# Attention of an adaLN block: slots of four heads at a time, with the probabilities turned by VectorE blocks and DRAM transfers instead of TensorE transposes

## The reference, cut to what matters

```python
mod = (silu(c) @ wmod).reshape(B, 6, 1, -1)          # sa, ca, ga, sb, cb, gb
h = layernorm(x) * (1 + ca) + sa
# attention: q, k with rotary embedding, causal softmax
scores = jnp.einsum('bhtd,bhsd->bhts', q, k) * (1.0 / np.sqrt(HD))
scores = jnp.where(tril, scores, -jnp.inf)
att = jax.nn.softmax(scores, axis=-1)
out = jnp.einsum('bhts,bhsd->bhtd', att, v)
x = x + ga * (out.transpose(0, 2, 1, 3).reshape(B, T, H * HD) @ wo)
h = layernorm(x) * (1 + cb) + sb
x = x + gb * (silu(h @ w1.T + b1) * (h @ w2.T + b2) @ w3.T + b3)
```

## Time and profile before

| | |
|---|---|
| median of 3 runs | 897.12 us (895.2 to 897.33) |
| the profiled execution, span from first to last instruction | 892.2 us |
| difference of the two (what lies around the span) | 4.9 us |
| TensorE (PE) busy | 870.8 us, 98% of the span |
| VectorE (DVE) busy | 590.9 us, 66% |
| ScalarE (ACT) busy | 509.9 us, 57% |
| GpSimd (POOL) busy | 465.4 us, 52% |
| moved by DMA | 38.22 MB, 43 GB/s on average |

### The profile page before, as it was taken

How to read it: one execution, slowest core, us unless ns; L and a number is a source line. 1 busy time by engine, 2 the same in 40 slices (tenths; PEclk the granted TensorE clock), 3 DMA queues, 4 the chain that set the end, 5 groups by cost and what they waited for, 6 DMA issues and landing times.

```text
span 892.2 us, 14536 instructions
## 1 busy us (share of the span) xinstructions
PE 870.8 (98%) x4716; PEld 744.8 (83%) x4716; DVE 590.9 (66%) x1693; ACT 509.9 (57%) x1194; POOL 465.4 (52%) x362
## 2 busy tenths in 40 slices
PE   8899999999999999999999999999999999998897
PEld 2798888888888888888888888888888887876786
DVE  4957756576656565666666565766565656788886
ACT  3657656575647475656656565756474656544410
POOL 1755745284537554563557462845475544525542
PEclk9999999999999999999999999999999999999999
DMA  9710101010101010101001010101010100111011
GB/s 330 229 46 1 60 1 60 1 61 1 59 0 59 0 59 0 35 24 51 8 0 59 0 59 0 59 0 59 0 47 0 71 1 26 58 72 24 1 48 47
DMA packets 27663, 38.22 MB, mean 43 GB/s; under 512 B 2416, under 2 KB 11760, under 8 KB 27632
## 3 DMA queue, kind: packets, MB, share of 16 engines
q1 hardware_dynamic: 27216, 37.76, 12.6%
q10 hardware_dynamic: 416, 0.07, 0.0%
HBM read 35.73 MB, written 2.10 MB: 42 GB/s over the span
## 4 chain that ended last, share of the span: by engine, by line
PE 90%; DVE 6%; ACT 2%; issue 1%; DMA 1%; SPq 0%; ACTq 0%; DVEq 0%
PE x_bank L311 27%; PE q_bank L311 19%; PE s_row L311 14%; PE o_bank L387 13%; PE t_col L373 6%; PE s_row L373 1%; PE s_row L611 1%; PE t_col L622 1%; PE q_bank L611 1%; PE x_bank L611 1%; DVE wo_raw L916 1%; DVE attn_lo L850 1%; PE x_bank L321 1%; PE x_bank L339 1%; DMA wmod_sb<-in_L_wmod_dram 1%
## 5 line engine op out<-in xcount | busy, mean ns | idle before, releaser
L1225 POOL TENSOR_TENSOR q_tmp<-q_tmp,sin_sb 128x512 f32<-128x512 f32 x64 | 87.6, 1369 | 274.4 <-ACT q_tmp L996 274.4
L987 ACT ACTIVATE probs<-probs,neg_max 128x128 f32<-128x128 f32 (+3 forms) x256 | 140.9, 561 | 4.0 <-DVE neg_max L673 2.1
L951 ACT ACTIVATE pT_hi<-t_col 128x512 fp32r<-128x512 f32 x128 | 69.6, 596 | 128.1 <-PE t_col L373 128.1
L668 DVE CUSTOM_DVE_ANT_0 probs<-s_row,mask_sb 128x256 f32<-128x256 f32 (+3 forms) x256 | 115.0, 486 | 4.1 <-issue 0.5
L694 DVE TENSOR_TENSOR attn_lo<-o_bank,attn_hi 128x512 fp32r<-128x512 f32 x64 | 44.2, 691 | 108.4 <-ACT attn_hi L951 108.3
L1203 POOL TENSOR_TENSOR qT_lo<-q_tmp,qT_hi 128x512 fp32r<-128x512 f32 x63 | 82.0, 1301 | 55.7 <-ACT qT_hi L951 55.7
L311 PE MATMUL q_bank<-hT_hi,wq_hi 128*128 128x512 f32 x256 | 105.3, 411 | 1.5 <-DVE q_tmp L658 1.5
L951 ACT ACTIVATE attn_hi<-o_bank 128x512 fp32r<-128x512 f32 x64 | 38.4, 599 | 119.6 <-PE o_bank L387 119.6
L311 PE MATMUL q_bank<-hT_hi,wq_lo 128*128 128x512 f32 x256 | 100.2, 392 | 0.0
L311 PE MATMUL q_bank<-hT_lo,wq_hi 128*128 128x512 f32 x256 | 100.2, 391 | 0.0
L311 PE MATMUL x_bank<-wo_hi,attn_hi 128*128 128x512 f32 x240 | 93.7, 390 | 0.1
(11 more groups left out here) (295 smaller groups left out, 2124.2 us busy)
## 6 DMA issues: line engine op xcount, KB each, us to landing
wo_raw<-in_L_attn_wo_dram SPq DMA_DIRECT2D x8, 1024.0 KB, 5.3
wq_raw<-in_L_attn_wq_dram SPq DMA_DIRECT2D x7, 1024.0 KB, 5.8
wmod_sb<-in_L_wmod_dram SPq DMA_DIRECT2D x6, 512.0 KB, 8.1
wmod_sb<-in_L_wmod_dram SPq DMA_DIRECT2D x3, 1024.0 KB, 13.5
wk_raw<-in_L_attn_wk_dram SPq DMA_DIRECT2D x8, 256.0 KB, 5.2
wv_raw<-in_L_attn_wv_dram SPq DMA_DIRECT2D x8, 256.0 KB, 6.0
wq_raw<-in_L_ffn_w_dram SPq DMA_DIRECT2D x2, 1024.0 KB, 5.3
out_dram<-acc SPq DMA_DIRECT2D x8, 256.0 KB, 2.1
```

What stands on the lines that cost most here:

```text
L668: last = nc.vector.tensor_tensor_reduce(probs[:, s, ROW_AT[i]:ROW_AT[i] + ROW_W[i]], s_out[i], mask_sb[:, T - ROW_W[i]:T], 1.0, LOWEST, AL ...
L951: nc.scalar.activation(dst, src, ACT.Copy).then_inc(done, 1)
L987: last = nc.scalar.activation(span, span, ACT.Exp, bias=neg_max[:, s, i:i + 1], scale=SCALE, accum_out=row_sum[:, s, i:i + 1])
L1225: nc.gpsimd.tensor_tensor(b, b, sin_sb[:, :], ALU.mult).then_inc(q_sin, 1)
```

## The change

A **slot** takes the place of the step: one tile of 128 queries, for all four heads of a group, of one batch entry. There are still 8 slots in a group and 64 in all; the query tiles come in the order 0, 3, 1, 2.

- **Scores.** q is stored as [dimension, block of 32 tokens, head, 32], so that the 128 stationary columns of a score matmul are 32 queries of each of the four heads. A slot has four such matmul triples, for the four blocks of 32 queries, against 32(4i+t+1) keys: the causal edge is cut at 32 columns instead of 128. The maxima write `probs` as [key block of 128, key chunk of 32, query block t, 32].
- **Turning.** One VectorE transpose per slot turns every 32x32 block of the slot's probabilities (`turn_blocks`). SP then writes the blocks to a DRAM buffer with four transfers (one per head, 32 partitions each), waits for them, and reads them back with one transfer in which the keys stand on 128 partitions. The read of slot s waits until `attend` of slot s-2 has let the buffer go.
- **Attend** of slot s-3 stands in slot s: three matmuls of 512 columns (four heads by 128 queries) for each key block. The output product of slot s-4 follows it.
- **Moved between engines.** The row normalisation goes from VectorE to ScalarE. The low part of the turned probabilities goes from VectorE to GpSimd. The rotary embedding loses ScalarE's two swapping copies and GpSimd's sine product; VectorE does three products (one of 128 partitions, two of 64 that read the other half). The negated maximum comes out of the maxima instruction itself, and the small memsets go.
- **Schedule.** The loop over groups is written out. Four q projections of the first group and one of batch entry 1, all turns of x and the six modulation pieces now stand before group 0. Raw weights share their place with the low parts, the weights come in more and smaller transfers.

The core of the diff:

```diff
-            def turn_probs(g, j, final=False):
-                need(pe, probs_normed, STEPS, g, j + 1)
-                ...
-                        for i in range(jj, TT):
-                            at = ROW_AT[i] + jj * P
-                            last = pe.transpose(t_out[jj][:, (i - jj) * P:(i - jj + 1) * P],
-                                                probs[:, j % 2, at:at + P], ident[:, :])
+            def scores(g, s):
+                b, i = s // TT, tile_of(s)
+                ...
+                for t in range(QT):
+                    need(pe, rows_maxed, QT * SLOTS, g, QT * (s - 1) + t + 1)
+                    n = width(s, t)
+                    product(s_banks[t][:, 0:n], lambda a, _: qT[a][b][:, QT * i + t, :, :],
+                            lambda a, _: kT[a][b][:, 0:n], [0]).then_inc(scores_ready, 1)
+            def attend(g, s):
+                b, i, par = s % SLOTS // TT, tile_of(s), s % 2
+                need(pe, attn_lo, SLOTS, g, s)
+                ...
+                    last = pe.matmul(o_bank[:, :], v_s[a][:, b, st_, :], pT[bb][par][:, :, PLACES[par] - 1 - i + st_, :],
+                                     start=(k == 0), stop=(k == len(steps) - 1))
+            def rotate(src, ring):
+                a, b = rope_tmp[:, ring, 0, :], rope_tmp[:, ring, 1, :]
+                nc.vector.tensor_tensor(a, src[:, :], cos_sb[:, :], ALU.mult)
+                nc.vector.tensor_tensor(b[0:HALF, :], src[HALF:HD, :], sin_sb[HALF:HD, :], ALU.mult)
+                nc.vector.tensor_tensor(b[HALF:HD, :], src[0:HALF, :], sin_sb[0:HALF, :], ALU.mult).then_inc(roped, 1)
+            def turn_blocks(g, s):
+                par, i = s % 2, tile_of(s)
+                need(dve, probs_normed, SLOTS, g, s + 1)
+                need(dve, blocks_out, MOVES * SLOTS, g, MOVES * s)
+                ...
+                nc.vector.transpose(dst, src).then_inc(blocks_turned, 1)
+            def blocks_to_dram(g, s):
+                par, i = s % 2, tile_of(s)
+                need(sp, blocks_turned, SLOTS, g, s + 1)
+                need(sp, pT_in[par], 16 * TT, g, 16 * (s // 2))
+                for h in range(REP):
+                    sp.dma_start(spread[par, :, :, h, 0:(i + 1) * P].rearrange("c s n -> s c n"),
+                                 turned[W32 * h:W32 * (h + 1), :, TT - 1 - i:, :].rearrange("p c a t -> p c (a t)")
+                                 ).then_inc(blocks_out, 16)
+            def blocks_to_keys(g, s):
+                par, i = s % 2, tile_of(s)
+                need(sp, blocks_out, MOVES * SLOTS, g, MOVES * (s + 1))
+                need(sp, attn_done, SLOTS, g, s - 1)
+                sp.dma_start(pT_raw[par][:, :, PLACES[par] - 1 - i:, :].rearrange("p h a t -> p h (a t)"),
+                             spread[par, :, :, :, 0:(i + 1) * P].rearrange("c s h n -> (c s) h n")).then_inc(pT_in[par], 16)
+            def normalise(g, s):                      # ScalarE
+                par = s % 2
+                need(act, inv_ready, SLOTS, g, s + 1)
+                for t in range(QT):
+                    rows = prob_rows(s, t)
+                    last = nc.scalar.activation(rows, rows, ACT.Copy, scale=row_inv[:, par, t:t + 1])
+                last.then_inc(probs_normed, 1)
+            def probs_low(g, s):                      # GpSimd
+                ...
+                    split_lo(pT[1][par][:, :, at, :], pT_raw[par][:, :, at, :], pT[0][par][:, :, at, :], pT_lo)
-            with pe.Fori(1, KV - 1) as g:
+            for g in range(1, KV - 1):
                 group(g)
```

More of the change, by code:

```diff
@@ new lines, in project_out @@
+            def project_out(g, s, x_free=None):
+                need(pe, attn_lo, SLOTS, g, s + 1)
+                need(pe, wo_added, SLOTS, g, s - 1)
+                dst = x_bank if s % 2 else out_bank
+                for h in range(REP):
+                    if s % SLOTS == 0:
+                        need(pe, wo_lo, REP, g, h + 1)
+                    for a, bb in PARTS:
+                        last = pe.matmul(dst[:, :], attn[a][:, s % 2, h * P:(h + 1) * P], wo_s[bb][:, h, :],
+                                         start=(h == 0 and (a, bb) == PARTS[0]), stop=(h == REP - 1 and (a, bb) == PARTS[-1]))
+                last.then_inc(wo_made, 1)
@@ L874, in _ @@
             group(0, first=True)
-            with dve.Fori(1, KV - 1) as g:
+            gates()
+            group(1)
+            for g in range(2, KV - 1):
                 group(g)
             group(KV - 1, last=True)
-            probs_low(KV - 1, STEPS - 1)
-            f_low(3)
+            end = KV - 1
+            add_out(end, SLOTS - 5)
+            attn_low(end, SLOTS - 3)
             f_low(4)
-            attn_low(KV - 1, STEPS - 1)
+            x1_stats(0)
+            x1_stats(1)
@@ L903, in _ @@
             for k in range(KC):
                 h2_low(k)
-            for u in range(9, 3 * KC):
-                f_low(u)
+            add_out(end, SLOTS - 1)
+            x1_stats(TT)
+            x1_stats(TT + 1)
             x1_stats(TT + 2)
```

1192 lines of the change are left out of this document (585 added, 607 removed).

## The result

The changed kernel takes 899.4 us, the kernel before 895.0 (medians of 20 runs each); the ratio is 1.0044, 95% interval 1.0032 to 1.0057. It is slower by about 4 us, where 825 us was forecast. One of the 20 runs of the changed kernel took 1326.6 us at a mean granted clock of 0.555 and has no part in the ratio. The profiled execution has a span of 896.0 us and a run time of 897.8.

What follows compares the result with a forecast made beforehand. The prediction took PE's issue time to bound attention: 892.2 us span less 93.4 of PE work gives 798.8, plus 21 for edges gives 819.8, with 4.9 around it 825 us; own range 804 to 850, 802 to 870 with rival 1.

Steps and rivals of the forecast that it cites:

- The work on TensorE: Per slot: transposes 1.09 us, attend 0.20 and scores 0.17 come off, 11.86 to 10.40; 93.4 us over 64 slots.
- The costs of the other engines: Work per slot: VectorE 6.8 us including 1.4 for the block transpose, ScalarE 6.5, GpSimd 7.8.
- Rival 3: Block transpose at the reciprocal's price: VectorE needs 13.8 us a slot, run about 1020 us; chance 4%.
- All fit below 10.40: Loop: VectorE, ScalarE and GpSimd each have less work per slot than TensorE's 10.40 us.
- edge (c): Loop: small stalls where GpSimd or ScalarE is behind (slot 3), 1 us a group, +7 us.
- rival 1: Loop: VectorE and ScalarE hand-overs become the bound, 11.0 to 11.3 us a slot, about 865 us; chance 25%.
- Edge (a): Start: work moved ahead of the first scores costs nothing in sum, but PE waits longer for VectorE's chain, +2 us.
- Edge (b): Group 0, slots 1 to 3: no attend or output product, PE has less work than the others, +5 us.
- Edges (d) and (e): Last group's slots 3 to 6 limited by the buffer's loop, +4 us; last attend waits for a full DRAM trip, +3.
- The trip through DRAM: Probabilities stored and reloaded: 10 to 12 us from transpose to landing, hidden in the loop, nearly bare in the last group.
- rival 2: The DRAM buffer's loop from attend to attend sets the pace: slot 12.8 us, about 965 us; chance 7%.
- What was said would show it wrong: PE's middle windows well below 97% busy; GpSimd's low part fed by late DMA as releaser would name rival 2.

Runs made afterwards that it cites:

- e6: The kernel before with only 3 of the 10 transposes of the probabilities per step in groups 1 to 7: 860.9 us, ratio 0.9620.
- e11: e1 with VectorE's block transpose of each slot done twice: 935.2 us, ratio 1.0477 to the kernel before.
- e1: The changed kernel with the high and low parts of wv's second half made in slot 4 instead of slot 5: 877.1 us.
- e2: The changed kernel with 8 unread 512-column matmuls added in slot 6 while TensorE waits for wv's low part: 885.9 us.
- e4: The changed kernel with 7 unread 512-column matmuls in the wait ahead of the transposes of x at 49 us: 893.0 us.
- e14: The changed kernel with the six modulation pieces ahead of the wait for x, two unread 512-column matmuls behind each: 893.1 us.
- e3: The changed kernel with the six modulation pieces spread between the prologue's projections instead of in one row: 885.9 us.
- e7: The changed kernel with e1's and e3's edits and, in the last group, the first gate's copy ahead of wo's high parts: 865.9 us.
- e8: e7 with gate operations split over two slots, last-group gate and weight turns behind attend, and low parts ahead of the second norm's small operations: 862.8 us.
- e5: The changed kernel with a DRAM-to-DRAM copy added between store and load of the probabilities: 940.3 us, ratio 1.0517 to the kernel before.
- e10: e1 with e5's added DRAM-to-DRAM copy: 936.3 us, ratio 1.0482 to the kernel before.
- e9: e8 with VectorE's output-product sum ahead of the maxima in alternate slots, gate operations one per slot, 8 unread matmuls in the tail's wait: 860.3 us.

## Why the prediction was wrong

- **The work on TensorE: right.** 1.46 us a slot was forecast, 93.4 in all; 88.5 came off, and the steady group has 84.0 us of work where 83.2 was said. Read by starts, a group has 14.1 us of scores (14.0 forecast) and 13.6 of attend (13.6). Of the transposes 8.07 us are gone, 1.01 a step and not 1.09: the slower start behind them, 0.08 a step, was counted as gone too, but the projections and the output product take 55.6 us a group, not less than the 55.4 before. In e6 a turn is worth the 0.109 us that the forecast had.
- **The costs of the other engines: right.** The block transpose takes 1.04 ns a column (2313 ns for 2048, 1.51 us a slot against 1.4); GpSimd's 7.8 us a slot is its 70% of 11.1; VectorE and ScalarE have 7.1 and 7.2 us against 6.8 and 6.5. Rival 3 falls. The Trainium skill's 311 ns ("VectorE: DVE Perf Modes", section "The three transpose paths") is for one 128x128 turn in bf16, a point that the prediction left out; ten times that, an estimate from the page's figure, is 3.1 us a slot, and the trace has 1.51 in float32. The four widths here (712, 1246, 1778 and 2313 ns for 512 to 2048 columns) lie on 0.18 us for each instruction plus 1.04 ns a column, which would give a lone turn of 128 columns 0.31 us, an estimate from these four: the page's figure itself is not contradicted, only multiplying it by the ten blocks of a long instruction.
- **"All fit below 10.40" was the failed step**, and with it edge (c): 1 us of stalls a group, where 4.7 us were lost in a steady one (3.0 of waits and 1.7 at half clock). I compared sums of busy time with the slot, and not where each result stands in its queue. wv's low part was in my sum (part of GpSimd's 1.55 us for weights) but I never asked which slot it is made in, what stands ahead of it, and who waits: project_v in slot 6. "Each semaphore has a slot or more of slack" was said of rival 1 without a row; e11 refutes it: adding 1.5 us a slot to VectorE, busy for 66% of the time, cost 6.3 us a group. How much of the loss this step explains: the steady groups, 23.6 us of the 92 in the table above, and a part of groups 0 and 1, where the same wait for wv stands (3.35 and 2.08 us). The rest are the steps below.
- **Rival 1 hit the loop's number by luck.** It gave 11.0 to 11.3 us a slot; measured is 88.67 / 8 = 11.08. But its cause was VectorE and ScalarE waiting for each other, and what e1 and e2 show is GpSimd's low part of wv (2.07 us a group) and the clock behind it (1.7); VectorE's sum is 0.7. Its 865 has neither the clock nor the ends.
- **The clock was in no term.** The earlier trace rows showed 1.00 before, because TensorE never rested, and I carried that over to a kernel in which I forecast rests. 38 of the 76 us missed are this. In the loop the wait of slot 6 is paid almost twice (2.07 + 1.7, e1 and e2); other waits of 2.0 and 2.8 us were paid once.
- **Edge (a), the start: 2 us forecast, 17 measured** (6.4 of waits and 10.5 at half clock; the moved work itself, 19.7 us at full clock, is as forecast). "Moved work ... costs nothing in sum" is the failed sentence. The pieces cost 1.70 us each when they stood alone between wide matmuls; in one row of six they take 2.9 (17.2 / 6), whether TensorE was idle before them or not (e4, e14). Spread, 10 to 13 us come back (e3). The wait for x's norm was 6.3 us, three times what I allowed.
- **Edge (b), groups 0 and 1.** 5 us were forecast for group 0, and it has 9.7 of waits and 6.8 at half clock: rotations (0.90 and 3.12 us), q's low part (1.26) and wv (3.35). Group 1 was in no edge but (c): the gates' row of small operations on VectorE was not in the sums by slot.
- **Edges (d) and (e), the end: 7 us forecast.** The last group and tail have 26.5 us of waits, all from 740 us on (5.70, 2.00, 2.36, 1.95, 2.83, 0.67, 6.70, 1.09, 3.17), and lose 9.2 at half clock; before it was 10.2 and 1.6, so 24 us came on top. The waits are not at attend for the trip as forecast, but at turns of gates and weights for ScalarE and VectorE, whose queues I had not followed past the change. That the shorter slots put them on the path is argued: e7's third edit and e8 moved them and won some 4 us together, so what the end can give back stays open.
- **The trip through DRAM: pieces about right, the whole longer, cover not proven.** Four stores take up to 2.8 us of SP and land mostly in 3 to 5, a load of 1 MB in 5.9. From the end of the transpose to the landing of the load the median of the 64 slots is 14.4 us against 10 to 12, and it goes up to 21, as SP also waits for buffers between the legs. TensorE waits 0.7 us in all for probabilities, so rival 2 falls for this kernel. But VectorE waits 27.8 us in all for the stores to free the one buffer, which the forecast didn't name, and e5 and e10 show no room for SP to be held longer.
- **What was said would show it wrong did:** the middle windows fell to 95 to 97% busy, and the releaser there was GpSimd's low part, but of wv, not of the probabilities. It would have named rival 2, which was not the cause.

## What to carry to other kernels

When the bound engine is relieved, the next bound is not the engine with the largest sum but the piece that stands latest in some in-order queue: for every producer of the bound engine, write down the slot it is made in, what stands ahead of it and when it is wanted. A forecast that allows idle time on TensorE must price the clock behind it: 1.7 us behind the wait of slot 6 here, nothing behind some others as long. Small cheap work that is moved can lose its price with its neighbours: 1.70 us a piece became 2.9. And work added to fill a wait must end with the wait, as e9's tail shows.

## What was not expected of the hardware

- A row of 2-column matmuls comes to run at half clock although TensorE has no gap: 96 of them take 16.9 us in e4, the first 4 us at a granted clock of 1.00, then at 0.50 (window 60 to 70), with the engine busy for 10.00 of 10 us. Alone, 16 take 1.84 us.
- Some tiny VectorE operations take seven times their time. Timeline of VectorE in the changed kernel, the second norm's statistics on 4 elements a partition, and then GpSimd's at the same time:

```profile
801.94 1.21 DVE L778 TENSOR_SCALAR rstd<-var_eps 128x4 int32<-128x4 int32 x1
803.18 1.18 DVE L780 TENSOR_TENSOR newton<-rstd 128x4 f32<-128x4 f32 x1
804.40 0.16 DVE L781 SCALAR_TENSOR_TENSOR newton<-newton,var_eps 128x4 f32<-128x4 f32 x1
804.59 1.11 DVE L782 SCALAR_TENSOR_TENSOR rstd<-newton,rstd 128x4 f32<-128x4 f32 x1
805.74 0.16 DVE L780 TENSOR_TENSOR newton<-rstd 128x4 f32<-128x4 f32 x1
```

```profile
801.87 1.26 POOL L1254 TENSOR_TENSOR acc<-acc,x_ring 128x512 f32<-128x512 f32 x1
803.08 1.26 POOL L1251 TENSOR_TENSOR acc<-acc,sin_sb 128x512 f32<-128x512 f32 x1
804.42 1.26 POOL L1254 TENSOR_TENSOR acc<-acc,x_ring 128x512 f32<-128x512 f32 x1
```

The slow ones end at 803.15, 804.36 and 805.70, the GpSimd operations beside them at 803.13, 804.34 and 805.68; once GpSimd has nothing more, all take 0.16 us. In the whole trace ten operations of this shape are slow, all with a GpSimd operation under way at their start and within 0.03 us of its end. But 26 others of this shape, reciprocals of the row sums, that run wholly within one of GpSimd's take 0.18 us. So it looks as if some kinds of small operation, and not all, wait for the end of GpSimd's; no run tested that. Here it puts 3 us on the chain of the second norm, behind which TensorE waited 6.70.
